# One unit fewer multiplied by seven products, and the residual rows requested in their own block

## The chip, the core and the metric
The kernel runs on one core of a Trainium2 chip. The metric is the device time of one execution in microseconds (us); the kernel before takes 782.37 us, the median of three runs (782.14 to 783.79).

## What is computed
Two graph layers over 4096 nodes with 256 features. `adj` is a dense 4096x4096 float32 matrix, and each layer multiplies all of it.

```
deg  = sum(adj, axis=1, keepdims=True) + 1e-5
out0 = relu((adj / deg) @ x @ W_neigh.T + b_neigh + x @ W_self.T + b_self)
x1   = layernorm(x + out0)
d    = rowsum(adj) ** -0.5                      # 0 where the sum is 0
out1 = relu((d[:, None] * adj * d[None, :]) @ x1 @ W + b)
out  = layernorm(x1 + out1)
```

## The kernel before, in words
Each layer is cut into `NB = 8` blocks of 512 output rows. A block is a sum over the 4096 nodes, taken in `NU = 16` units of 256 nodes. For a unit the queue of SyncE (SP) requests a tile of the transposed matrix, `raw`, 128x1024 float32 (512 KB), into a ring of four slots. ScalarE (ACT) rounds it to `hi`, VectorE (DVE) takes `lo = raw - hi` and TensorE (PE) multiplies in three passes: hi by hi, hi by the low part of the features, lo by hi. The sums of block b stand in `ps_main[b % 2]`. In the second layer the features are `z`, the scaled rows of the first layer; they lie in `zs` for the first 28 tiles and in `xs` for the last four.

A plain unit is 12 matmuls of 512 columns (L1079). In blocks 1 to 6 of the second layer the units in `SU` are multiplied another way (`seven_products`, L994): a unit is read as a 2x2 arrangement of quarters, and seven products of quarter sums replace eight products. That makes 21 matmuls of 256 columns: nine at L1017 on `hi`, `lo` and precomputed sums of the features, and twelve at L1026 on sums of the quarters of `raw`. Those sums cost work on DVE and ACT:

- `s_sums` and `s_last_sum`: four additions over 128x256 on DVE (L738, L739, L741, L745). They stand two units ahead of the unit that they serve, so that the sums for unit 3 are made in unit 1.
- `s_hi`: the rounding of the sums on ACT (128x1024, L359, shown as `xs<-acc`), and `s_lo`: their low part on DVE (L567, `xs<-acc,xs`).
- Of `raw` itself only three quarters are split (128x768 in place of 128x1024).
- Once, in block 0 of the second layer: `t_sums`, `t_hi`, `t_lo` make the feature sums for two units at a time, at units 5, 8, 11 and 14 for seven units.

Some of the products belong to two quarters; they gather in `ps_epi` and are joined to the columns in the next block. There, while PE works on units 0 to 4, ACT copies them out (`take_own`, L382, after unit 2's `hi`), DVE makes four additions (`join_own`, L690 to L697) and one over 128x1024 (`join_columns`, L704), ACT rounds the joined columns (`st_hi`), and DVE takes their low part (`st_lo`). In DVE's program `join_columns` stands ahead of unit 3's `lo`, and `st_lo` right behind it. PE's product with the weights of the block before (L958) stands behind unit 3 and again behind unit 5. The rest of the block before (bias, residual, layer norm, store) follows in units 6 to 15; its store is issued by ACT in unit 15. In the code a block's epilogue is always run inside the next block.

Everything on an engine runs in program order. Waits are on semaphores that only count up. SP requests the tile of unit u once DVE has made the `lo` of unit u - 4 (`l_ready`), ACT makes the `hi` of unit u once PE is done with unit u - 4 (`unit_done`). The residual rows of a block, 512 KB from DRAM into `res`, are requested by `load_residual` (L281): at unit 2 of the next block, behind that unit's tile and ahead of the tile of unit 3. In the second layer the request waits until the first layer's eight stores have landed. `res` is read in units 6 to 9 of the next block.

Of the kernel before, what the change touches and what calls it, by code (L numbers as in the profile page):

```python
# [29 lines left out]
NB = N // IB  # L30
TB = IB // P
UJ = 2
NU = JT // UJ
# [4 lines left out]
ZOWN = JT - TB  # L38
# [1 line left out]
HT = TB // 2  # L40
TAIL = NU - RING
WARM = 10
SU = tuple(range(1, 14, 2))
NS = len(SU)
SUMS_AT = tuple(max(u - 2, 0) for u in SU)
SRING = 2
T_AT = XC + FH
T_UNITS = tuple(range(5, 16, 3))
S_AT = T_AT + 2 * NS
QP = 32  # L50
QS = IB // QP
# [5 lines left out]
def build(nc, x_nat, xt_in, adj_in, wn_in, bn_in, ws_in, bs_in, w1_in, b1_in, out):  # L57
    f32 = mybir.dt.float32
    f32r = mybir.dt.float32r
    bf16 = mybir.dt.bfloat16  # L60
    ALU = mybir.AluOpType
# [4 lines left out]
    with ctx:  # L66
        def sb(name, shape, dt=f32):
            return ctx.enter_context(nc.sbuf_tensor(name, shape, dt))

        def sem(name):  # L70
            return ctx.enter_context(nc.semaphore(name))
# [4 lines left out]
        zs = sb("zs", [P, ZOWN, 2, F], f32r)  # L76
# [47 lines left out]
        z_joined, t_chain, t_ready = sem("z_joined"), sem("t_chain"), sem("t_ready")  # L124
# [5 lines left out]
        tt_stored = sem("tt_stored")  # L130
# [20 lines left out]
        def slot(u):  # L151
            return u % RING

        def is_last(e):

            return isinstance(e, int) and e == NB - 1

        def is_first(b):
            return isinstance(b, int) and b == 0
# [5 lines left out]
        def x_stage(c):  # L165

            if c == 0:
                return acc[:, 1, :].rearrange("p (t f) -> p t f", t=XC)
            return (res, tt)[c % 2][:, :, :]

        def w_stage(i):

            return acc[:, 1, i * IB:(i + 1) * IB].rearrange("p (k f) -> p k f", k=FH)

        def wait_x_split(eng, c):

            eng.wait_ge(xl_ready, c + 1)
# [14 lines left out]
        def by_seven(layer, b):  # L192

            return layer == 1 and not isinstance(b, int)
# [14 lines left out]
        def s_index(b, parity, u):  # L209

            return b * NS + (SU.index(u) - NS)

        def s_slot(parity, u):

            return ((0 if parity == 1 else NS) + SU.index(u)) % SRING

# [40 lines left out]
        @block.sync  # L257
        def _(sp):
            def load_x(c):
                if c >= 3:  # L260
                    wait_x_split(sp, c - 2)
                sp.dma_start(x_stage(c), x_nat[c]).then_inc(x_full[c % 2], 16)

            def load_weights():
                sp.wait_ge(unit_done, WHOLE)
                wait_x_split(sp, 0)
                sp.dma_start(w_stage(1), ws_in).then_inc(ws_full, 16)
                sp.dma_start(w_stage(0), wn_in).then_inc(wn_full, 16)

            def load_biases():  # L270
                for dst, src in ((bias0, bn_in), (bias1, b1_in)):
                    sp.dma_start(dst[:, :], src.rearrange("(a n) -> a n", a=1).to_broadcast([P, F]))\
                      .then_inc(bias_full, 16)

            def load_xt(b, u):
                if u != (9 if is_first(b) else 3):
                    return

                sp.dma_start(xt[:, :, :], xt_in[b]).then_inc(xt_full, 16)

            def load_residual(layer, e):  # L281


                if layer == 1:
                    sp.wait_ge(tt_stored, (NB + 1) * 16)
                rows = x_nat[e] if layer == 0 else x1_dram[e].rearrange("t p f -> p t f")
                sp.dma_start(res[:, :, :], rows).then_inc(res_full, 16)

            def one_block(layer, b, parity, epi):
                g0 = b * NU + layer * NB * NU  # L290
                for u in range(NU):
                    if epi is None and u == 0:
                        sp.dma_start(raw[:, 0, :], adj_in[0, 0]).then_inc(raw_full[0], 16)
                        continue
                    if not (epi is None and u < RING):

                        if epi is None and u - RING < WHOLE:
                            sp.wait_ge(unit_done, u - RING + 1)
                        else:
                            sp.wait_ge(l_ready, g0 + (u - RING + 1))  # L300
                        if layer == 0 or (is_first(b) and u < RING):
                            sp.wait_ge(acc_done, g0 + (u - RING + 1))
                    sp.dma_start(raw[:, slot(u), :], adj_in[b, u]).then_inc(raw_full[slot(u)], 16)
                    if layer == 0:
                        load_xt(b, u)
                    if epi is None:
                        if u % 2 == 1 and 1 < u < NU - 1:
                            load_x((u + 1) // 2)
                        if u == 8:
                            load_weights()  # L310
                        if u == 12:
                            load_biases()
                    elif layer == 1 and is_last(b) and u == 8:

                        sp.wait_ge(c_ready, NB - 1)
                        sp.dma_start(w1_raw, w1_in[:, FH - 1, :]).then_inc(w1_full, 16)
                    elif u == 2:
                        load_residual(*epi)
                        if layer == 1 and is_first(b):

                            sp.dma_start(xt[:, :, 0:F], w1_in).then_inc(w1_full, 16)

            def last_epilogue(epi):
                load_residual(*epi)
                for t in range(HT):
                    sp.wait_ge(x1_ready, (2 * NB - 1) * TB + t + 1)
                    sp.dma_start(out[NB - 1, t], tt[:, t, :]).then_inc(tt_stored, 16)
                sp.wait_ge(y_ready, 1)
                sp.dma_start(out[NB - 1, HT], tt[:, HT, :]).then_inc(tt_stored, 16)

                sp.wait_ge(tt_stored, (2 * NB + TB) * 16)

            layers(sp, one_block, last_epilogue)

        @block.gpsimd
# [20 lines left out]
        def _(act):  # L356
# [21 lines left out]
            def take_own(e, parity):  # L378

                act.wait_ge(own_zeroed, 1)  # L380
                act.wait_ge(unit_done, (e + NB) * NU + (SU[-1] + 1))
                act.activation(own_sbuf[:, :, :], ps_epi[:, parity * HT:(parity + 1) * HT, :], ACT.Copy).then_inc(own_ready, 1)  # L382
# [8 lines left out]
            def s_hi(b, parity, u):  # L391
                act.wait_ge(s_ready, s_index(b, parity, u) + 1)
                split_hi(s_part(0, parity, u), acc[:, s_slot(parity, u), :]).then_inc(sh_ready, 1)
# [48 lines left out]
            def one_block(layer, b, parity, epi):  # L442
                g0 = b * NU + layer * NB * NU
                k0 = b * (NU // RING) + layer * NB * (NU // RING)
                for u in range(NU):
# [25 lines left out]
                    if not (epi is None and u < RING):  # L471
                        act.wait_ge(unit_done, g0 + (u - RING + 1))
                    by_7 = by_seven(layer, b) and u in SU
                    cols = slice(0, UW - HB if by_7 else UW)
# [5 lines left out]
                    if by_7:  # L480
                        s_hi(b, parity, u)
                    if layer == 1 and is_first(b) and u in T_UNITS:
                        t_hi(T_UNITS.index(u))
                    if epi is not None:
# [68 lines left out]
        def _(dve):  # L553
# [152 lines left out]
            def t_sums(j):  # L706

                gs = t_group(j)
                m = len(gs)
                tiles = zs[:, 4 * gs[0]:4 * gs[-1] + 4].rearrange("p (g i) c f -> p g i c f", i=4).bitcast(f32)  # L710
                z = acc[:, 0, 0:m * IB].rearrange("p (g q f) -> p g q f", q=UJ, f=F)
                t = acc[:, 1, 0:m * IB].rearrange("p (g k f) -> p g k f", k=4, f=P)
                b11, b12, b21, b22 = z[:, :, 1, 0:P], z[:, :, 1, P:F], z[:, :, 0, 0:P], z[:, :, 0, P:F]
                t1, t2, t3, t4 = [t[:, :, k, :] for k in range(4)]
                dve.tensor_tensor(z, tiles[:, :, 2:4, 0, :], tiles[:, :, 2:4, 1, :], ALU.add).then_inc(z_joined, 1)
                dve.wait_ge(z_joined, j + 1)
                dve.tensor_tensor(t3, b22, b12, ALU.subtract).then_inc(t_chain, 1)
                dve.tensor_tensor(t1, b12, b11, ALU.subtract).then_inc(t_chain, 1)
                dve.wait_ge(t_chain, 3 * j + 1)
                dve.tensor_tensor(t2, t3, b11, ALU.add).then_inc(t_chain, 1)  # L720
                dve.wait_ge(t_chain, 3 * j + 3)
                dve.tensor_tensor(t4, b21, t2, ALU.subtract).then_inc(t_ready, 1)
# [71 lines left out]
            def one_block(layer, b, parity, epi):  # L794
# [8 lines left out]
                for u in range(NU):  # L803
# [26 lines left out]
                    if layer == 1 and is_first(b):  # L830
                        if u in T_UNITS:
                            t_lo(T_UNITS.index(u))
                        if u + 1 in T_UNITS:
                            t_sums(T_UNITS.index(u + 1))
                        if u == NU - 1:
# [340 lines left out]
```

## Time and profile before

| | us |
|---|---|
| median of 3 runs | 782.37 |
| profiled execution, its own time | 785.61 |
| its span in the trace | 783.9 |
| PE busy | 771.1 (98%) |
| DVE busy | 706.4 (90%) |
| ACT busy | 424.9 (54%) |

The span runs from the first to the last instruction; 1.7 us of the profiled execution lie around it. The granted TensorE clock is full (a mean of 0.997) except at the two ends. Matmuls are pipelined, so the duration of one (391 ns for 512 columns) is longer than the distance between the starts of two. How long a unit takes on PE is read from start to start. The second layer begins on PE near 401 us; its blocks take some 46 us each.

### The profile page before, as it was taken

How to read it: one execution, taken by the hardware profiler on the slowest of the kernel's cores; microseconds unless marked ns; L12 is line 12 of the kernel's file. 1: busy time of each engine (PE TensorE's matmuls, PEld its weight loads, DVE VectorE, ACT ScalarE, POOL GpSimd, SP SyncE). 2: the span in 40 equal slices, each digit the busy share in tenths (PEclk: the TensorE clock that was granted, in tenths of full speed). 3: DMA queues.
4: the chain of work that ended last, by engine and by line, in shares of the span. 5: the costliest groups of instructions: out<-in, count | busy, mean ns of one | idle time of the engine just before them, and what ended most of it. 6: DMA issues, size and time to landing. Idle time of an engine off the chain costs nothing.

```text
span 783.9 us, 12545 instructions
## 1 busy us (share of the span) xinstructions
PE 771.1 (98%) x4106; PEld 661.3 (84%) x4106; DVE 706.4 (90%) x1193; ACT 424.9 (54%) x590; POOL 2.5 (0%) x14
## 2 busy tenths in 40 slices
PE   9999999999999999999999999999999999999996
PEld 6888888888888888888888789798888989898886
DVE  6999999999899998998979899798989989898654
ACT  5644644646356463454535756556565665657452
POOL 0000000000000000000000000000000000000000
PEclk9999999999999999999999999999999999999998
DMA  7966574756647456474674556658465574847741
GB/s 300 335 231 202 199 253 156 248 190 202 226 161 247 171 201 237 142 247 177 199 242 145 197 176 208 216 164 267 161 214 209 186 245 162 268 161 215 259 149 54
DMA packets 54205, 161.08 MB, mean 205 GB/s; under 512 B 5024, under 2 KB 18080, under 8 KB 54176
## 3 DMA queue, kind: packets, MB, share of 16 engines
q1 hardware_dynamic: 45680, 151.54, 57.4%
q10 hardware_dynamic: 8352, 9.05, 3.4%
q8 instruction: 16, 0.26, 0.1%
q0 software_dynamic: 144, 0.13, 0.1%
q14 instruction: 13, 0.11, 0.1%
HBM read 152.31 MB, written 8.39 MB: 205 GB/s over the span
## 4 chain that ended last, share of the span: by engine, by line
PE 55%; DVE 25%; issue 10%; DMA 5%; ACT 4%; DVEq 1%; ACTq 0%; SPq 0%
PE ps_main L1079 45%; DVE lo L567 7%; PE ps_epi L958 6%; DVE xs L567 5%; DMA raw<-adj_t 3%; ACT hi L359 2%; DVE acc L741 2%; DVE acc L848 1%; PE ps_main L1101 1%; DVE tt L623 1%; DVE acc L738 1%; DVE ps_main L704 1%; DVE tt L639 1%; DMA tt<-x_nat 1%; ACT tt L406 1%
## 5 line engine op out<-in xcount | busy, mean ns | idle before, releaser
L359 ACT ACTIVATE hi<-raw 128x1024 fp32r<-128x1024 f32 x254 | 255.5, 1018 | 147.6 <-PE ps_main L1079 98.6
L567 DVE TENSOR_TENSOR lo<-raw,hi 128x1024 fp32r<-128x1024 f32 x254 | 297.4, 1174 | 29.0 <-ACT hi L359 28.9
L1079 PE MATMUL ps_main<-hi,xs 128*128 128x512 f32 x1120 | 278.9, 391 | 0.4 <-DVE xs L681 0.4
L1079 PEld LDWEIGHTS ps_main<-hi,xs 128*128 128x128 f32 x1120 | 207.3, 188 | 42.5 <-DVE xs L681 0.8
L1079 PE MATMUL ps_main<-lo,xs 128*128 128x512 f32 x560 | 149.7, 389 | 0.0
L848 DVE TENSOR_TENSOR acc<-acc,raw 128x1024 f32<-128x1024 f32 x112 | 136.3, 1217 | 0.0
L1079 PE MATMUL ps_main<-hi,zs 128*128 128x512 f32 x544 | 135.6, 391 | 0.0
L1079 PEld LDWEIGHTS ps_main<-lo,xs 128*128 128x128 f32 x560 | 105.1, 188 | 21.9
L1079 PEld LDWEIGHTS ps_main<-hi,zs 128*128 128x128 f32 x544 | 99.5, 188 | 18.9
L359 ACT ACTIVATE xs<-acc 128x1024 fp32r<-128x1024 f32 (+1 forms) x47 | 49.3, 1049 | 73.0 <-DVE acc L745 60.7
L1079 PE MATMUL ps_main<-lo,zs 128*128 128x512 f32 x272 | 72.7, 389 | 0.0
L567 DVE TENSOR_TENSOR xs<-acc,xs 128x1024 fp32r<-128x1024 f32 (+1 forms) x47 | 56.7, 1206 | 6.9 <-ACT xs L359 6.9
L1026 PE MATMUL ps_epi<-xs 128*128 128x256 f32 x378 | 62.5, 283 | 0.0
L1079 PEld LDWEIGHTS ps_main<-lo,zs 128*128 128x128 f32 x272 | 51.1, 188 | 10.6
L1026 PEld LDWEIGHTS ps_epi<-xs 128*128 128x128 f32 x378 | 54.3, 192 | 0.0
L406 ACT ACTIVATE tt<-tt,nmr,inv_root 128x256 f32<-128x256 f32 x60 | 32.6, 591 | 26.6 <-DVE nmr L676 26.6
L1026 PE MATMUL ps_main<-xs,zs 128*128 128x256 f32 x126 | 36.8, 292 | 2.8 <-ACT xs L359 1.5
L400 ACT ACTIVATE ps_epi<-tt,nmean 128x256 f32<-128x256 f32 x48 | 22.5, 468 | 29.9 <-DVE nmean L645 29.9
L359 ACT ACTIVATE st_hi<-ps_main 128x1024 fp32r<-128x1024 f32 (+1 forms) x18 | 16.5, 919 | 36.5 <-DVE ps_main L704 26.5
L1026 PEld LDWEIGHTS ps_main<-xs,zs 128*128 128x128 f32 x126 | 24.1, 191 | 5.0 <-DVE xs L567 2.5
L639 DVE SCALAR_TENSOR_TENSOR tt<-tt,res 128x256 f32<-128x256 f32 x64 | 26.5, 417 | 0.0
L567 DVE TENSOR_TENSOR st_lo<-ps_main,st_hi 128x1024 fp32r<-128x1024 f32 (+1 forms) x18 | 19.6, 1090 | 7.3 <-ACT st_hi L359 6.9
(157 smaller groups left out, 784.8 us busy)
## 6 DMA issues: line engine op xcount, KB each, us to landing
raw<-adj_t SPq DMA_DIRECT2D x256, 512.0 KB, 3.5
res<-x_nat SPq DMA_DIRECT2D x11, 512.0 KB, 6.1
xt_sb<-xt SPq DMA_DIRECT2D x8, 512.0 KB, 6.4
x_scratch<-tt ACTq DMA_DIRECT2D x8, 512.0 KB, 4.1
res<-x_scratch SPq DMA_DIRECT2D x8, 512.0 KB, 6.1
out<-tt ACTq DMA_DIRECT2D x7, 512.0 KB, 7.4
tt<-x_nat SPq DMA_DIRECT2D x3, 512.0 KB, 4.6
acc<-x_nat ACTq DMA_DIRECT2D x1, 512.0 KB, 4.9
```

The lines of the kernel that those rows point to most:

```text
L359: return act.activation(dst, src, ACT.Copy)
L400: act.activation(tile_sums(layer, e, parity, t)[:, 0:F], tt[:, t, :], ACT.Square, bias=nmean[:, t:t + 1], accum_out=squares[:, t:t + 1]).t ...
L406: act.activation(tt[:, t, :], tt[:, t, :], ACT.Identity, bias=nmr[:, t:t + 1], scale=rstd[:, t:t + 1]).then_inc(x1_ready, 1)
L567: return dve.tensor_tensor(dst, src, hi_part.bitcast(f32), ALU.subtract)
L623: ins = dve.scalar_tensor_tensor(out=tt[:, t, :], in0=sums[:, 0:F], scalar=(rdeg, d_cur)[layer][:, t:t + 1], in1=(bias0, bias1)[layer][:, ...
L639: link(dve.scalar_tensor_tensor(out=tt[:, t, :], in0=tt[:, t, :], scalar=0.0, in1=res[:, t, :], op0=ALU.max, op1=ALU.add, accum_out=sums[: ...
L704: dve.tensor_tensor(columns, columns, own, ALU.add).then_inc(c_ready, 1)
L741: dve.tensor_tensor(s2, a22, s3, ALU.subtract).then_inc(s_chain, 1)
L848: dve.tensor_tensor(a, a, raw[:, slot(v), :], ALU.add).then_inc(acc_done, 1)
L958: last = pe.matmul(ps, st[:, k, rows], weight(part, k), start=(k == 0 and q == 0), stop=(k == FH - 1 and q == 2))
L1026: last = pe.matmul(ps, st(part), mov[:, at * HB:(at + 1) * HB], start=(ps is p5 and first and i == 0), stop=(n > 0 and last_s and i == 2), ...
L1079: last = pe.matmul(ps[:, f, :], stationary(layer, part, jt, f), mov[:, slot(u), cols], start=(jt == 0 and i == 0), stop=(jt == JT - 1 and ...
```

## The change
Unit 3 leaves `SU`, so that six units of a block go by seven products and unit 3 is plain. `SUMS_AT` follows from `SU`: no sums are made in unit 1 any more. The feature sums have three groups of two units (5, 8, 11) and no fourth, and `t_sums` picks its tiles by the units in `SU`, which are no longer evenly spaced. In the second layer the residual rows of block b are requested at unit 14 of block b itself, behind the tile of unit 14 and ahead of the tile of unit 15. In block 0 that request waits for seven of the first layer's stores, not eight. The last block's rows too are requested at its unit 14.

```diff
-SU = tuple(range(1, 14, 2))
+SU = (1, 5, 7, 9, 11, 13)
-T_UNITS = tuple(range(5, 16, 3))
+T_UNITS = tuple(range(5, 5 + 3 * ((NS + 1) // 2), 3))
...
-            def load_residual(layer, e):
+            def load_residual(layer, e, stored=NB):
                 if layer == 1:
-                    sp.wait_ge(tt_stored, (NB + 1) * 16)
+                    sp.wait_ge(tt_stored, (stored + 1) * 16)
...
-                    elif u == 2:
+                    if layer == 1 and u == NU - 2:
+
+                        load_residual(layer, b, NB - 1 if is_first(b) else NB)
+                    elif u == 2 and epi is not None and epi[0] == 0:
                         load_residual(*epi)
-                        if layer == 1 and is_first(b):
+                        if layer == 1:
                             sp.dma_start(xt[:, :, 0:F], w1_in).then_inc(w1_full, 16)
             def last_epilogue(epi):
-                load_residual(*epi)
...
-                tiles = zs[:, 4 * gs[0]:4 * gs[-1] + 4].rearrange("p (g i) c f -> p g i c f", i=4).bitcast(f32)
+                first, last = SU[gs[0]] * UJ, SU[gs[-1]] * UJ
+                step = last - first if m == 2 else UJ
+                at = 0 if first + m * step <= ZOWN else step - UJ
+                tiles = zs[:, first - at:first - at + m * step].rearrange("p (g i) c f -> p g i c f", i=step)\
+                    .bitcast(f32)[:, :, at:at + UJ]
...
-                dve.tensor_tensor(z, tiles[:, :, 2:4, 0, :], tiles[:, :, 2:4, 1, :], ALU.add).then_inc(z_joined, 1)
+                dve.tensor_tensor(z, tiles[:, :, :, 0, :], tiles[:, :, :, 1, :], ALU.add).then_inc(z_joined, 1)
```

On DVE, at the start of a block of the second layer's loop, from unit 1's `s_lo` (`xs<-acc,xs`) on, before:

```order
L567 TENSOR_TENSOR xs<-acc,xs 128x1024
L738 TENSOR_TENSOR acc<-raw 128x256
L739 TENSOR_TENSOR acc<-raw 128x256
L740 ISA
L741 TENSOR_TENSOR acc<-raw,acc 128x256
L744 REGISTER_ALU
L745 TENSOR_TENSOR acc<-raw,acc 128x256
L821 REGISTER_ALU
L567 TENSOR_TENSOR lo<-raw,hi 128x1024
L690 TENSOR_TENSOR xt_sb<-xt_sb 128x256
L692 ISA
L693 TENSOR_TENSOR xt_sb<-xt_sb 128x256
```

The same place now (`xt_sb` is where the joined products are gathered; L692 is the first of the four additions of the join):

```order
L569 TENSOR_TENSOR xs<-acc,xs 128x1024
L827 REGISTER_ALU
L569 TENSOR_TENSOR lo<-raw,hi 128x1024
L692 TENSOR_TENSOR xt_sb<-xt_sb 128x256
L694 ISA
L695 TENSOR_TENSOR xt_sb<-xt_sb 128x256
L697 TENSOR_TENSOR xt_sb<-xt_sb 128x256
```

The four sums for unit 3, which read the tile of unit 3, are gone from between `s_lo` of unit 1 and `lo` of unit 2.

On SP, in the block ahead of the second layer's loop (block 0), from the first residual request on, before:

```order
L287 DMA res<-x_nat 128x1024
L321 DMA xt_sb<-w 128x2x256
L303 DMA raw<-adj_t 128x1024 x13
L251 UNCONDITIONAL_BRANCH
L251 ISA
```

The same place now:

```order
L287 DMA res<-x_nat 128x1024
L324 DMA xt_sb<-w 128x2x256
L303 DMA raw<-adj_t 128x1024 x12
L287 DMA res<-x_scratch 128x4x256
L303 DMA raw<-adj_t 128x1024
L251 UNCONDITIONAL_BRANCH
L251 ISA
```

The request of the block's own residual rows (`x_scratch` is the first layer's result) stands ahead of the last tile, where the loop's first block had it behind its third.

## Rows read from the trace of the kernel before

**Rows 1.** Page: busy time of PE; median landing of a tile.

```profile
PE   771.1 (98%) x4106; PEld 661.3 (84%) x4106; DVE 706.4 (90%) x1193; ACT 424.9 (54%) x590; POOL 2.5 (0%) x14
...
raw<-adj_t SPq DMA_DIRECT2D x256, 512.0 KB, 3.5
```

**Rows 2.** Timeline of PE (start, us, operation): unit 0 in blocks 1, 2, 3, 6, 7.

```profile
448.88 1.98 PE L1079 MATMUL ps_main<-hi,zs 128*128 128x512 f32 x8
...
496.16 1.98 PE L1079 MATMUL ps_main<-hi,zs 128*128 128x512 f32 x8
...
543.79 1.98 PE L1079 MATMUL ps_main<-hi,zs 128*128 128x512 f32 x8
...
681.83 1.98 PE L1079 MATMUL ps_main<-hi,zs 128*128 128x512 f32 x8
...
727.35 1.98 PE L1079 MATMUL ps_main<-hi,zs 128*128 128x512 f32 x8
```

**Rows 3.** Timeline of PE: units 12, 13, 14 of block 1 begin.

```profile
485.43 2.00 PE L1079 MATMUL ps_main<-hi,zs 128*128 128x512 f32 x8
487.27 1.07 PE L1079 MATMUL ps_main<-lo,zs 128*128 128x512 f32 x4
488.18 0.28 PE L1017 MATMUL ps_epi<-hi,zs 128*128 128x256 f32 x1
...
490.69 2.00 PE L1079 MATMUL ps_main<-hi,xs 128*128 128x512 f32 x8
```

**Rows 4.** Timeline of PE: unit 3 of block 2, product behind it; then block 6.

```profile
504.14 0.28 PE L1017 MATMUL ps_epi<-hi,zs 128*128 128x256 f32 x1
...
505.98 0.38 PE L1017 MATMUL ps_epi<-lo,zs 128*128 128x256 f32 x1 [0.97 <-DVE lo L567]
...
507.12 0.39 PE L1026 MATMUL ps_main<-xs,zs 128*128 128x256 f32 x1 [0.53 <-ACT xs L359]
...
509.15 0.40 PE L958 MATMUL ps_epi<-xs,st_hi 128*128 128x256 f32 x2
...
689.81 0.28 PE L1017 MATMUL ps_epi<-hi,zs 128*128 128x256 f32 x1
...
692.70 0.40 PE L958 MATMUL ps_epi<-xs,st_hi 128*128 128x256 f32 x2
```

**Rows 5.** Timeline of DVE: units 0 to 3 of block 2.

```profile
492.51 1.23 DVE L567 TENSOR_TENSOR lo<-raw,hi 128x1024 fp32r<-128x1024 f32 x1 [1.62 <-ACT hi L359]
...
499.54 0.42 DVE L738 TENSOR_TENSOR acc<-raw 128x256 f32<-128x256 f32 x1 [1.99 <-DMA raw<-adj_t]
...
501.01 1.22 DVE L567 TENSOR_TENSOR lo<-raw,hi 128x1024 fp32r<-128x1024 f32 x1
...
504.98 0.95 DVE L567 TENSOR_TENSOR lo<-raw,hi 128x768 fp32r<-128x768 f32 x1
506.15 1.22 DVE L567 TENSOR_TENSOR st_lo<-ps_main,st_hi 128x1024 fp32r<-128x1024 f32 x1 [0.23 <-ACT st_hi L359]
```

**Rows 6.** Chain that ended last, in order of time: tile of unit 3.

```profile
491.05 8.47 DMA raw<-adj_t
```

**Rows 7.** Timeline of SP: tile of unit 15, block 1; residual request in block 2.

```profile
481.25 0.33 SPq L303 DMA_DIRECT2D raw<-adj_t  x1
...
489.39 0.39 SPq L287 DMA_DIRECT2D res<-x_scratch  x1
```

**Rows 8.** Timeline of ACT: unit 15's hi, block 1.

```profile
488.58 1.04 ACT L359 ACTIVATE hi<-raw 128x1024 fp32r<-128x1024 f32 x1
```

**Rows 9.** Block 0's end: PE at unit 14; ACT's rounding of feature sums.

```profile
443.26 2.14 PE L1079 MATMUL ps_main<-hi,xs 128*128 128x512 f32 x8 [0.42 <-DVE xs L681]
...
438.59 0.63 ACT L359 ACTIVATE xs<-acc 128x512 fp32r<-128x512 f32 x1 [0.34 <-DVE acc L722]
```

**Rows 10.** DMA issues in 486 to 500 us (KB, us to landing).

```profile
out<-tt ACTq DMA_DIRECT2D x1, 512.0 KB, 11.3
```

**Rows 11.** The last block: SP's residual request; unit 15's hi on ACT.

```profile
755.00 0.43 SPq L287 DMA_DIRECT2D res<-x_scratch  x1
...
763.16 1.06 ACT L359 ACTIVATE hi<-raw 128x1024 fp32r<-128x1024 f32 x1 [0.68 <-PE ps_main L1079]
```

## The prediction
> **What bounds the kernel now.** I read the busy times first. PE is busy for 771.1 of 783.9 us, DVE for 706.4 [rows 1]: PE sets the time, and only two things can change it, how long PE needs for its matmuls and how long it stands still. DVE at 90% is close behind, so it can be late at single places. Next I took PE's timeline and followed the starts of unit 0 through the second layer, since a block must take the same time whenever PE is not held up. They lie at 448.88, 496.16, 543.79, 681.83 and 727.35 us in blocks 1, 2, 3, 6 and 7 [rows 2]. So block 1 takes 47.28, block 2 takes 47.63, blocks 3 to 5 together 138.04 (46.01 each), block 6 takes 45.52. The same work takes up to 2.1 us longer in one block than in another: that is standstill.
>
> Then, where it stands still. A group by seven products takes 488.18 to 490.69 = 2.51 us when nothing holds it [rows 3]. Unit 3 of block 2 starts at 504.14 and the product behind it at 509.15: 5.01 us, so 2.50 lost. PE waited for the `lo` of unit 3, then for ACT's rounding of the sums, then for their low part [rows 4]. In block 6 the same unit takes 692.70 - 689.81 = 2.89, so 0.38 lost [rows 4]. Taking that off, a block without standstill is 45.52 - 0.38 = 45.14 us. The six blocks 1 to 6 take 727.35 - 448.88 = 278.47, the floor is 6 x 45.14 = 270.84: 7.6 us are lost, by block 2.1, 2.5, then 2.6 in three blocks, and 0.4. In block 2 the loss is all in unit 3, since 47.63 - 2.50 = 45.13 is the floor again.
>
> Why DVE is late there is in its own timeline [rows 5]. Behind unit 1's work it wants the four sums for unit 3, whose tile has not landed: it stands for 1.99 us, until 499.54. The sums take it to 501.01. Then come unit 2's `lo`, the join, unit 3's `lo` at 504.98 and `st_lo` at 506.15. PE wanted that `lo` about 0.7 us after 504.14. The tile landed 8.47 us after its request at 491.05 [rows 6], against a median of 3.5 [rows 1]; ahead of it in SP's queue stood the 512 KB of residual rows, requested at 489.39 [rows 7], and beside it ran the store of the block before, which took 11.3 us [rows 10].
>
> **The change part by part.** *Unit 3 plain, cost on PE.* A plain unit takes 488.18 - 485.43 = 2.75 us, a seven-product unit 2.51 [rows 3]. Six blocks, one unit each: 6 x 0.24 = +1.4 us. It is certain, because PE has no idle time for it to hide in. The Trainium skill has a rule that would make this dearer ("TensorE: Matmul & The Clock Gate", Back-to-back issue gap: a warm matmul starts N/2.4 + 2.5 ns after the one before): 12 x 216 against 21 x 109 ns are 2.59 and 2.29 us, a difference of 0.30, so +1.8 in all, an estimate from that page. The rows of this case show 229 and 120 ns from start to start, and I go by them.
>
> *Unit 3 plain, what it takes off.* Per block DVE loses four sums, 501.01 - 499.54 = 1.47 us [rows 5], and one 1.2 us low part, and gains 0.27 (1.22 in place of 0.95 for `lo`); ACT loses one rounding. Idle time or work of DVE alone is worth nothing; what counts is when PE gets its inputs. In block 2 the sums (1.47) and the wait in front of them (1.99) fall away from between 492.51 and 506.15, so `st_lo` begins at about 506.15 - 3.46 = 502.7 and ends at 503.9. The `lo` of unit 3 is done at about 502.7. The plain unit needs its `lo` only behind its first eight matmuls, 1.84 us after its start [rows 3], so at 504.14 + 1.84 = 505.98, and the product behind it needs `st_lo` at 504.14 + 2.75 = 506.9. Both are there with 3.0 us to spare. In block 6 there is no wait to drop, only the 1.47, and it is ample for a loss of 0.38. So the standstill at unit 3 goes in all six blocks: -7.6 us. What is late next: the `lo` of unit 4 and the sums for unit 5, which now stand 3.5 us earlier as well, and PE comes to unit 4 only after a 1.4 us product. I book nothing.
>
> *The residual request moved.* In a block's first units the queue now carries tiles only, so the tile of unit 3 should land sooner than 8.47 us; nobody needs it before ACT's `hi` and DVE's `lo` of unit 3. In block 1 the request also waited for a store of the first layer, with the tile of unit 3 queued behind it; that wait goes. These are part of the 7.6 and count once. The price is at the new place: behind the request stands the tile of unit 15 and then those of the next block. In block 1 the tile of unit 15 is requested at 481.25 and ACT takes it at 488.58 [rows 7, 8]. With the request's 0.39 us in front it has 6.9 us to land without anybody noticing. The nearest rows are 3.5 at the low end and 8.47 for a tile behind residual rows and beside a store; the store is not running at unit 14, so I take 6 to 7, and a cost of nothing. If it were 8.47, `hi` and all that follows on DVE would be 1.6 us late, inside the 3.0 us of room at unit 3. The last block: its tile of unit 15 is requested just ahead of 755.00 and taken at 763.16 [rows 11], 8 us; even at 8.47 the `lo` half of that unit is not yet wanted. Nothing. The residual rows themselves land some 20 us before they are read.
>
> *The fourth group of feature sums.* It is gone from block 0: five small DVE operations, one rounding on ACT of 0.63 us that DVE held up by 0.34, and its low part. They stood ahead of the scaling of the last feature rows, for which PE waits 0.42 us at unit 14 [rows 9]. That wait goes or nearly: -0.4; at worst 0.
>
> *Sum.* -7.6 - 0.4 + 1.4 = -6.6 us in the profiled execution: 785.61 becomes 779.0. That execution is 3.2 us above the median of 782.37. The losses beyond the smallest depend on how late a tile lands, so part of the 3.2 may be standstill that ordinary runs do not have, and that the change then cannot take away. By bounds: if they have all of it, 782.37 - 6.6 = 775.8. If only block 1 keeps its 2.1 and the others have the mean of blocks 3 to 6, (2.6 + 0.4)/4 = 0.75, the loss is 5.9 and the gain 4.9: 777.5. If all six have 0.75, the loss is 4.5, the gain 3.5: 778.9. I take a gain of 5.4: **777.0 us**, with 775.3 to 779.0 as this case's own range.
>
> **Rivals.** *A: DVE stays late around the join.* The waits for tiles go, but the join chain still ends late, because ACT comes later with `take_own` or `hi` than I assume, and PE loses the 0.75 per block elsewhere in units 3 to 5. For it: DVE is at 90%, and every block without a late tile still lost something. Against it: the 1.47 us fewer are more than those losses, and a plain unit asks for its `lo` 1.1 us later. Time: -6.6 + 6 x 0.75 = -2.1, 780.3.
>
> *B: slower, by the tile of unit 15.* The residual rows go ahead of it in the same queue. If it lands L us after its request, ACT is L - 6.9 late, and DVE's whole start of the next block with it; unit 3 takes up 3.0, and the rest is PE's loss in each of six blocks. To eat up the gain of 6.6 it must lose 1.1 per block: the point is L = 11.0. At the 11.3 us that the store took in this trace [rows 10], 1.4 per block are lost, 8.4 in all: +1.8, 784.2. Against it: that store is another kind of transfer, at the fullest moment of the block, and tiles behind residual rows took 8.47 there. The Trainium skill says that descriptors are consumed in ring order on each DMA engine ("DMA: Bandwidth & Descriptors", Queues, rings and completion order), so the later tile has to let the rows through first; the trace's 8.47 us is in line with it.
>
> *C: no change.* DVE's lateness was only where it showed, and PE, freed at unit 3, meets it again later in the block, at units 13 to 15, say. Then of the 7.6 all but the 1.4 for the plain unit comes back: within 1 us, 781.5 to 783.4. Against it: behind unit 3 PE never waited, though DVE was 2 to 3 us later than it will be.
>
> **How the numbers follow.** Main case 0.80, A 0.11, B 0.04, C 0.05. What a measurement of this kernel can tell from no change is about 0.2%, 1.6 us, so faster begins below 780.8. The main case is faster throughout; A is on the faster side but near the bound, 0.07 to 0.04 between faster and same; C is same (0.04) or slower (0.01), B slower. Faster 0.87, same 0.08, slower 0.05. The range of 775.2 to 780.2 takes the bounds of the main case and part of the way to A.
>
> **What would show it.** Right: the starts of unit 0 in blocks 1 to 7 lie 45.4 us apart (45.14 + 0.24), evenly; unit 3 is 12 matmuls at 2.75 us with no releaser beside it; DVE no longer waits for a tile in unit 1 or 2, and `st_lo` ends 2 to 3 us before the product. Wrong: a wait of PE at units 4 or 5 (A); hi of unit 15 released by a DMA and blocks over 46 us (B); waits of PE near the end of the block (C); or a median gain of under 3 us with even blocks in the profile, which would say that ordinary runs did not have the loss.

## The result: 0.56% faster, and the profile after

The changed kernel takes 778.91 us, the median of 5 runs (778.44 to 779.27), against 782.35 for the kernel before, measured beside it: a ratio of 0.9944 with a 95% interval of 0.9932 to 0.9957. In a later session the kernel before took 784.33 us and the changed one 778.54, a ratio of 0.9928 (0.9914 to 0.9942). The changed kernel hardly varies; the one before does.

The profiled execution went from 785.61 to 778.69 us, its span from 783.9 to 777.0. From the page of the changed kernel, busy times and the chain that ended last:

```profile
PE 769.2 (99%) x4052; PEld 659.7 (85%) x4052; DVE 692.2 (89%) x1157; ACT 425.1 (55%) x583; POOL 2.5 (0%) x14
...
PE 99%; DVE 0%; ACT 0%; issue 0%
```

In the page of the kernel before that chain reads:

```profile
PE 55%; DVE 25%; issue 10%; DMA 5%; ACT 4%; DVEq 1%; ACTq 0%; SPq 0%
```

PE's timeline after the change, unit 0 of blocks 0, 1, 2, 3 and 7 of the second layer, which answers to [rows 2]:

```profile
401.74 1.98 PE L1085 MATMUL ps_main<-hi,zs 128*128 128x512 f32 x8
...
448.41 1.98 PE L1085 MATMUL ps_main<-hi,zs 128*128 128x512 f32 x8
...
493.75 1.98 PE L1085 MATMUL ps_main<-hi,zs 128*128 128x512 f32 x8
...
539.09 1.98 PE L1085 MATMUL ps_main<-hi,zs 128*128 128x512 f32 x8
...
720.45 1.98 PE L1085 MATMUL ps_main<-hi,zs 128*128 128x512 f32 x8
```

Blocks 1 to 6 all take 45.34 us, to the hundredth: 720.45 - 448.41 = 272.04 for the six, against 278.47 before. That is 6.43 of the 6.9 us. Block 0 takes 46.67; before it began at 401.45 and took 47.43, so another 0.76. The first layer ended 0.3 later; it is the same in every kernel here and ends between 401.4 and 402.8 us, so that is chance.

DVE's timeline in units 0 to 3 of block 2, which answers to [rows 5], and the start of PE's unit 3 and of the product behind it, for [rows 4]:

```profile
487.31 1.23 DVE L569 TENSOR_TENSOR lo<-raw,hi 128x1024 fp32r<-128x1024 f32 x1 [1.62 <-ACT hi L361]
...
496.29 1.22 DVE L569 TENSOR_TENSOR lo<-raw,hi 128x1024 fp32r<-128x1024 f32 x1
497.48 1.22 DVE L569 TENSOR_TENSOR st_lo<-ps_main,st_hi 128x1024 fp32r<-128x1024 f32 x1
```

```profile
501.73 1.98 PE L1085 MATMUL ps_main<-hi,zs 128*128 128x512 f32 x8
...
504.45 0.40 PE L964 MATMUL ps_epi<-xs,st_hi 128*128 128x256 f32 x2
```

The tile of unit 15, now behind the residual rows in the queue, landed like this in block 1 (KB, us from issue), which answers to [rows 7]:

```profile
raw<-adj_t SPq DMA_DIRECT2D x1, 512.0 KB, 6.7
```

`st_lo` is done at 498.7, 5.8 us before PE's product wants it; I had worked out 3.0. The difference stands at the block's start: DVE begins unit 0 at 487.31, 6.4 us ahead of PE (493.75). Before, it was 3.65 ahead (492.51 and 496.16) [rows 2, 5]. DVE did not only get rid of work in unit 1, it came into the block earlier.

### The profile page after: what moved, and what is told of

The parts are those of the page before. It is cut to its first block, busy times and chain, and to the rows that moved or that the text cites. A ratio compares the mean times of both kernels' runs of the same rounds, so it can differ in the third digit from the quotient of the medians.

```text
span 777.0 us, 12364 instructions
## 1 busy us (share of the span) xinstructions
PE 769.2 (99%) x4052; PEld 659.7 (85%) x4052; DVE 692.2 (89%) x1157; ACT 425.1 (55%) x583; POOL 2.5 (0%) x14
## 4 chain that ended last, share of the span: by engine, by line
PE 99%; DVE 0%; ACT 0%; issue 0%
PE ps_main L1085 75%; PE ps_epi L964 7%; PE ps_epi L1032 5%; PE ps_main L1023 3%; PE ps_main L1032 2%; PE ps_epi L1023 2%; PE ps_main L1107 1%; PE ps_main L964 1%; PE ps_main L1060 1%; PE ps_main L1045 1%; PE ps_epi L1117 0%; DVE tt L625 0%; PE ps_epi L985 0%; DVE tt L641 0%; ACT ps_epi L513 0%; ACT tt L527 0%
## 5 line engine op out<-in xcount | busy, mean ns | idle before, releaser
L361 ACT ACTIVATE hi<-raw 128x1024 fp32r<-128x1024 f32 x254 | 260.6, 1028 | 215.0 <-PE ps_main L1085 150.3
L1085 PE MATMUL ps_main<-hi,zs 128*128 128x512 f32 x592 | 147.4, 391 | 0.0
L1085 PEld LDWEIGHTS ps_main<-hi,zs 128*128 128x128 f32 x592 | 108.5, 188 | 20.9
L1085 PE MATMUL ps_main<-lo,zs 128*128 128x512 f32 x296 | 79.1, 389 | 0.0
L569 DVE TENSOR_TENSOR xs<-acc,xs 128x1024 fp32r<-128x1024 f32 x40 | 48.9, 1221 | 7.1 <-ACT xs L361 7.1
L361 ACT ACTIVATE xs<-acc 128x1024 fp32r<-128x1024 f32 x40 | 42.1, 1053 | 23.5 <-DVE acc L751 11.3
L1032 PE MATMUL ps_epi<-xs 128*128 128x256 f32 x324 | 53.4, 283 | 0.0
L1032 PEld LDWEIGHTS ps_epi<-xs 128*128 128x128 f32 x324 | 46.7, 192 | 0.0
L1032 PE MATMUL ps_main<-xs,zs 128*128 128x256 f32 x108 | 30.6, 283 | 0.0
L964 PE MATMUL ps_epi<-ws_sb,st_hi 128*128 128x256 f32 x128 | 23.6, 282 | 0.0
```

Source lines behind the costliest of these rows:

```text
L361: return act.activation(dst, src, ACT.Copy)
L569: return dve.tensor_tensor(dst, src, hi_part.bitcast(f32), ALU.subtract)
L964: last = pe.matmul(ps, st[:, k, rows], weight(part, k), start=(k == 0 and q == 0), stop=(k == FH - 1 and q == 2))
L1032: last = pe.matmul(ps, st(part), mov[:, at * HB:(at + 1) * HB], start=(ps is p5 and first and i == 0), stop=(n > 0 and last_s and i == 2), ...
L1085: last = pe.matmul(ps[:, f, :], stationary(layer, part, jt, f), mov[:, slot(u), cols], start=(jt == 0 and i == 0), stop=(jt == JT - 1 and ...
```

## The experiments

**The kernel before, profiled again.** It is unchanged.

> The kernel before, unchanged, profiled once more: its first profile was 785.61 us, its ordinary runs are 782.3. Theory T: what the ordinary runs do not have is standstill at unit 3 for late tiles. Then this profile shows blocks 1 to 6 of the second layer 45.1 us plus a loss of 0.4 to 1 us each (2.1 in block 1), about 4.5 in all, not 7.6, and a span near 780.7. Rival: the 3.3 us lay elsewhere (start, first layer), and the loss at unit 3 is 7.6 again with a shorter span.

Measured: 783.24 us, span 781.5. Units 0 of blocks 1 and 7:

```profile
449.09 1.98 PE L1079 MATMUL ps_main<-hi,zs 128*128 128x512 f32 x8
...
725.00 1.98 PE L1079 MATMUL ps_main<-hi,zs 128*128 128x512 f32 x8
```

275.91 us for six blocks, so 5.1 lost over 6 x 45.14 in place of 7.6. The 2.5 us less are the 2.4 that this execution is faster than the first profile. I had expected about 4.5 us of loss and a span near 780.7. So the two executions differ by the standstill in these blocks, and the first profile had caught much of it. But the ordinary runs beside this one had a median of 784.52 us (783.47 to 785.02): it lies 1.3 us below them, where the first profile lay 3.2 above its own. And the standstill is not all that varies: the first layer's end moves by up to 1.4 us, and kernels whose blocks are even in the profile still have runs up to 2.2 us apart (below).

**The request alone, and the plain unit alone.** The first undoes the change of `SU` (and with it the groups of feature sums), the second undoes the move of the request.

```diff
 # seven_units_res_moved, against the changed kernel
-SU = (1, 5, 7, 9, 11, 13)
+SU = (1, 3, 5, 7, 9, 11, 13)
 # plain_res_at_unit_2, against the changed kernel
-                    if layer == 1 and u == NU - 2:
-                        load_residual(layer, b, NB - 1 if is_first(b) else NB)
-                    elif u == 2 and epi is not None and epi[0] == 0:
+                    if u == 2 and epi is not None:
                         load_residual(*epi)
...
             def last_epilogue(epi):
+                load_residual(*epi)
```

> The residual request alone is moved; unit 3 stays with seven products. Theory T (DVE's sums for unit 3 in unit 1 keep it late at the join): PE still waits 0.4 to 0.75 us in unit 3 of each block; against the changed kernel -1.4 for the cheaper unit, +0.4 for the feature sums, +2.4 to 4.5 of standstill: 780.3 to 782.4. Rival R (the standstill came from the late tile, so the moved request alone does it): no waits, blocks 45.1 us apart, 777.9.

> Unit 3 is plain, the residual request stays at unit 2 of the next block. Theory T: without sums in unit 1 nobody needs the tile of unit 3 before DVE has joined, so a late tile is hidden; blocks 45.34 us apart, 778.9 as the changed kernel. Rival R (the late tile is the cause): one or two blocks still lose 1 to 2 us, block 1 among them, 780 to 782.

| kernel | median us | ratio to before (784.52) | blocks 1 to 6, us each |
|---|---|---|---|
| request moved, unit 3 by seven | 781.02 | 0.9957 (0.9944 to 0.9971) | 45.30, 45.55, 45.87, 45.54, 45.83, 45.53 |
| unit 3 plain, request at unit 2 | 778.85 | 0.9931 (0.9917 to 0.9944) | 45.34 in all six |

The plain unit alone does everything: every block at 45.34, and the same time as the whole change. A tile is still late in its block 1, where ACT stands 2.1 us for it, and costs nothing. The request alone is worth 3.5 us in the kernel with seven units, chiefly in block 1 (45.30 us, against 46.86 in the repeated profile), where SP had waited 6.5 us in the first profile for a store of the first layer, and nothing that can be seen once the unit is plain. The two were one gain, not two. With the request moved DVE waits for no tile any more, and yet five of the six blocks lose 0.4 to 0.7 us: that part was never a matter of tiles.

**One more plain unit.** `SU = (1, 5, 9, 11, 13)`.

> The changed kernel with unit 7 plain too (five units by seven products). Theory T: PE sets the time everywhere, so each further plain unit costs 0.23 us in each of six blocks: blocks 45.57 us apart, 778.9 + 1.4 = 780.3. Rival: DVE is still part of the bound somewhere and its relief pays for it, 778.9 or less.

Measured: 779.88 us (778.87 to 780.81), all six blocks 45.52 us. Theory T holds and prices the exchange: 0.18 us per unit and block (I had expected 0.23), where 0.20 separates 45.34 from the 45.14 of a block with seven products in seven units and no wait (below). The single rows of one unit had given 0.24 [rows 3].

**More work on DVE.** Four, then three reductions ahead of unit 2's `lo`, their result unused.

```diff
+                        for i in range(4 if by_seven(layer, b) and u == 2 else 0):     # 3 in the other
+                            dve.tensor_reduce(spare[:, i:i + 1], raw[:, slot(u), :], AX.X, ALU.add)
                         split_lo(lo[:, slot(u), cols], raw[:, slot(u), cols], hi[:, slot(u), cols]).then_inc(l_ready, 1)
```

> The changed kernel with four reductions over 128x1024 (some 1.15 us each, result unused) on DVE ahead of unit 2's lo in blocks 1 to 6: 4.6 us more in front of the join. By the prediction's 3.0 us of room PE loses 1.6 us in each of six blocks: 788. By the 5.8 us of the changed kernel's trace it loses nothing at unit 3: 779, at most 781 if DVE, then busy for 44.5 of 45.3 us, comes late elsewhere.

> The changed kernel with three reductions (3.4 us) on DVE ahead of unit 2's lo in place of four. Theory L (DVE is bound by its own round: 40.0 us of work a block and 3.1 us of waits that its order forces, so 43.1 in 45.34, and whatever is over 45.34 lengthens the block): 40.0 + 3.1 + 3.4 = 46.5, so blocks of 46.5 us, 1.2 more each, 786. Theory S (room at the join, 5.8 us by the trace): no loss, 779. The prediction's 3.0 us of room: 0.4 a block, 781.3.

Measured: 790.89 us with four (1.0083, 1.0068 to 1.0099) and 783.66 with three (0.9992, 0.9981 to 1.0004). Neither room was right. With 4.6 us more, less than the 5.8 of room, the first block lost 1.2 us and the others 2.1 to 2.4; with three the first lost nothing and the others 1.0 to 1.3. The first block lives on the lead it brings along; after that each block is a round that DVE can't finish in time. To see this I took DVE's own rounds, from the start of unit 0's `lo` to the same place one block later, here from block 3 to block 4. The columns are length, PE, PEld, DVE, ACT, POOL, granted clock, DMA share, GB/s, for the kernel before, the changed one, three more, four more:

```profile
540.44:585.96 45.52, 45.29 (x279) 40.61 (x278) 42.07 (x79) 27.51 (x39) 0.00 (x0) 1.00 0.62 202
```

```profile
532.82:577.81 44.99, 44.99 (x270) 40.15 (x269) 39.99 (x73) 27.62 (x37) 0.00 (x0) 1.00 0.64 207
```

```profile
537.07:583.37 46.30, 45.53 (x270) 40.06 (x269) 43.11 (x76) 26.78 (x38) 0.00 (x0) 1.00 0.63 202
```

```profile
539.35:586.79 47.44, 45.84 (x270) 39.99 (x269) 44.25 (x78) 26.78 (x38) 0.00 (x0) 1.00 0.61 199
```

And what DVE waited for in block 3 of the kernel before:

```profile
DVE lo L567 <- ACT hi L359: 2.5, 2, 1.6
DVE xs L567 <- ACT xs L359: 0.3, 1, 0.3
DVE st_lo L567 <- ACT st_hi L359: 0.2, 1, 0.2
```

Length less DVE's work is 3.45, 5.00, 3.19 and 3.19 us. In the two slowed kernels and in the one before it is what DVE has to wait in any case, some 3 us at places where its order makes it wait for ACT (two of them at units 15 and 0, where ACT is busy with the block's norm and its store), and a few tenths between instructions. Only in the changed kernel is it more, because there DVE waits for PE as well: its rounds of 45.0 and 45.5 us alternate around PE's 45.34, and its lead at the block's start stays at 6.3 to 6.6 us. In every other round one of the waits for ACT is 0.3 us longer, so that rounds of two lengths alternate: 45.52 and 45.85 us with seven units and the request moved, 46.30 and 46.65 with three reductions, 47.4 and 47.8 with four. These are the lengths of PE's blocks too. So the kernel before was on DVE's round even in the blocks with no late tile, and a late tile was added to the round directly: the rounds that hold a wait for a tile of 1.99 and of 0.7 us take 47.93 and 46.65 us. Theory L gave 46.5 for three; measured 46.3 to 46.65, though its total of 786 forgot the first block's lead.

**Two more transfers in front of the tile of unit 15.**

```diff
                         load_residual(layer, b, NB - 1 if is_first(b) else NB)
+                        for i in range(2):
+                            sp.dma_start(spare[i, b], x_nat[b]).then_inc(spare_full, 16)
```

> The changed kernel with two further 512 KB copies (DRAM to DRAM, of rows of x, read by nobody) behind the residual request at unit 14 of each block of the second layer, ahead of the tile of unit 15. That is rival B on purpose: the tile, which now lands in 6.7 us, should land in 11 to 13. By the prediction's room (6.9 us unnoticed, then 3.0 at unit 3) blocks 1 to 6 are 1 to 3 us longer, 785 to 797. By the room that the changed kernel's trace shows (low part of the joined columns done 5.8 us before PE's product) the blocks stay within 0.3 us of 45.34: 779 to 781.

Measured: 778.92 us (777.74 to 779.97), every block at 45.34. The tile was late for ACT, which waited 2.0 us for it in block 1:

```profile
486.36 1.06 ACT L367 ACTIVATE hi<-raw 128x1024 fp32r<-128x1024 f32 x1 [2.00 <-DMA raw<-adj_t]
```

but it landed 7.2 us after its own request at 479.06, itself held back by the others. Counted from 0.65 us after the residual request at 476.54, where the change alone puts it, that is some 9 us, not 11 to 13. So the run shows that about 2 us of lateness there cost nothing, and does not tell my two rooms apart. Rival B is far from the changed kernel, whose tile landed in 6.7 us.

**Back to seven units, in another order.** Against the kernel with seven units and the request moved: at unit 3 ACT and DVE take the sums of the unit before the joined columns; the four groups of feature sums stand where `T_UNITS` says.

```diff
-T_UNITS = tuple(range(5, 5 + 3 * ((NS + 1) // 2), 3))      # (5, 8, 11, 14) for seven units
+T_UNITS = (5, 8, 10, 12)      # seven_units_all_hidden; also (3, 5, 8, 11) and (4, 6, 8, 11)
 ACT:
+                    if by_7:
+                        s_hi(b, parity, u)
                     if epi is not None and epi[0] == 1 and u == 3:
                         joined_columns(epi[1], 1 - parity)
-                    if by_7:
-                        s_hi(b, parity, u)
 DVE:
+                    if by_seven(layer, b) and u == 3:
+                        s_lo(b, parity, u)
                     place(u, 1)
                     if by_seven(layer, b):
-                        if u in SU:
+                        if u in SU and u != 3:
                             s_lo(b, parity, u)
```

> Seven units and the moved request, with one order changed at unit 3: ACT rounds the sums of unit 3 before the joined columns, DVE takes their low part before that of the joined columns. Theory: what is left of the standstill in that kernel (0.2 to 0.7 us a block) is PE waiting for the low part of the sums behind st_lo; then it goes, blocks 45.14 us apart: 781.0 - 2.8 = 778.2. Rival: DVE is simply full at the block's start, and the wait turns up at the product behind unit 3 or at the next units: 780.5 to 781.

> As the one before, and the four groups of feature sums at units 5, 8, 10 and 12 of block 0 in place of 5, 8, 11 and 14. Theory: block 0 of the second layer is 47.4 us long with a group at unit 14 and 46.67 without; with the group earlier it is 46.67 again: 0.7 less than the one before, 777.5, and 1.4 under the changed kernel. Rival: the groups crowd DVE in units 8 to 12 of block 0 and PE waits there: no gain.

> Seven units, request moved, the sums of unit 3 taken first, and the four groups of feature sums at units 3, 5, 8 and 11 of block 0, so that none stands in front of the norm of the last rows. Theory: blocks 1 to 6 at 45.14 to 45.3, block 0 at 46.67 with no wait for the last z rows: 777.4 to 777.9, at least 1 us under the changed kernel. Rival: a group at unit 3 meets the first layer's last block there, and PE waits in units 3 to 5 of block 0: 778.5 or more.

> The same with groups at units 4, 6, 8 and 11. Theory: as the one before, 777.4 to 777.9. Rival: three groups two units apart cost DVE 6.4 us in each pair of units of 5.4 us, and its lead runs out by unit 8: a wait of PE of 1 us or more in block 0.

> The changed kernel once more, beside the other kernels of this chip: 778.9, blocks 1 to 6 at 45.34 us, block 0 at 46.67.

| kernel | median us | ratio to before of its session | block 0 | blocks 1 to 6 |
|---|---|---|---|---|
| sums first, groups 5, 8, 11, 14 | 779.13 | 0.9932 (0.9918 to 0.9946) | 47.41 | 45.14 to 45.52 |
| groups 5, 8, 10, 12 | 781.94 | 0.9968 (0.9957 to 0.9979) | 50.90 | 45.14 |
| groups 3, 5, 8, 11 | 777.59 | 0.9916 (0.9902 to 0.9930) | 46.67 | 45.14 |
| groups 4, 6, 8, 11 | 777.57 | 0.9916 (0.9902 to 0.9930) | 46.67 | 45.13 to 45.34 |
| the changed kernel again | 778.54 | 0.9928 (0.9914 to 0.9942) | 46.66 | 45.34 |

The order alone takes away most of the standstill: in the first of these block 3 is 45.17 us long with the same seven units, against 45.85 in the kernel before:

```profile
539.45:584.62 45.17, 45.17 (x280) 40.81 (x279) 41.95 (x79) 27.61 (x39) 0.00 (x0) 1.00 0.67 212
```

PE no longer waits there behind `st_lo` for the sums' low part, and DVE no longer waits 0.2 us for `st_hi`. The six blocks lose 0.55 us together in place of 2.8; I had booked the whole 2.8, and 778.2 us. What is left has the same reason as before. DVE's rounds are shorter by 0.3 us only, 45.2 and 45.5 in turn, which is still more than the 45.14 that PE needs. The kernel with groups 3, 5, 8, 11 hides this, since DVE comes into block 2 with a lead of 5.5 us in place of 3.6. DVE's unit 0 in its blocks 2 and 7 (PE's stand at 493.65 and 719.35):

```profile
488.13 1.23 DVE L569 TENSOR_TENSOR lo<-raw,hi 128x1024 fp32r<-128x1024 f32 x1 [1.62 <-ACT hi L361]
...
714.81 2.36 DVE L569 TENSOR_TENSOR lo<-raw,hi 128x1024 fp32r<-128x1024 f32 x2 [1.64 <-ACT hi L361]
```

Over five rounds the lead falls from 5.5 to 4.5 us: DVE needs 45.34 us a round, PE takes 45.14. In the kernel with sums first and groups 5, 8, 11, 14 the blocks begin to lose at a lead near 3.2 us. By my estimate, from 5.5 at 0.2 a round, this one would be there after some twelve rounds, and seven units would then be no better than six, whose blocks take 45.34 as well.

The feature sums were a matter of place: at unit 14 they cost 0.75 us and part of DVE's lead; at units 10 and 12, where I had expected 777.5 us, they pushed the first layer's last norm back and PE stood still for 2.4 us; early in the block they cost nothing. The last three rows come from one chip. Seven units in this order, with the groups early, are the fastest kernel of the study, by 0.95 us of median over the changed one; the intervals overlap, but the blocks show where it comes from, 6 x 0.20 = 1.2 us.

## Why the prediction was right, and where not

The forecast was 777.0 us (775.2 to 780.2); measured 778.91. The gain of the profiled execution, 6.9 us, was forecast as 6.6; that of ordinary runs, 3.4, as 5.4.

- *Unit 3 plain, +1.4.* Right in kind, a little large: +1.2, from 45.14 to 45.34 in six blocks. The formula of the Trainium skill ("TensorE: Matmul & The Clock Gate", Back-to-back issue gap) would have made it 1.8; the blocks do not agree. The Trainium skill gives that formula there for one matmul by itself and says that at 512 columns it counts too much, which I had left out. The rows of this case have it the other way: 229 ns from start to start against its 216 [rows 3].
- *The standstill at unit 3, -7.6.* It went entirely in the profiled execution: PE waits at no unit of blocks 1 to 6. The sum came out, but only in part for the reason that I gave: see the cause below.
- *Sizing it for ordinary runs.* This is the term that was off. I put the gain between 3.5 and 6.6 and took 5.4; in the first session it was 3.4, just under my lower bound. (The 775.3 at the lower end of this case's own range follows from none of the bounds; the lowest that I worked out is 775.8.) The loss over the floor was 5.1 us in the repeated profile, and in the ordinary runs of the first session, by 3.4 + 1.2 - 0.76, some 3.9. In the later session, with 5.8 us of gain, it would by the same sum be 6.2; no profile of these ordinary runs shows it. One profile of this kernel is a sample of something that varies by 2 us and more.
- *The cause of the lateness.* Half right. I named the late tile and, with it, the moved request as part of the 7.6. The tile explained what came on top in blocks 1, 2 and 4, where DVE waited 1.9, 2.0 and 0.7 us for it, but the plain unit alone gives all the gain. "Idle time or work of DVE alone is worth nothing" failed: DVE's round was the bound in these blocks, 42.1 us of work and some 3.5 to 3.8 of waits and gaps that its order forces. With unit 3 plain the work is 40.0 us a round, 2.1 less (I had 2.4), and the wait for `st_hi` goes. That brought the round under PE's 45.34 us, with room for a late tile besides, and was the change's whole effect. The order of the work was worth nearly as much, as the last experiment shows.
- *3.0 us to spare at unit 3.* Measured 5.8, since I shortened DVE's path inside one block and left its start where it was. And neither number is room for more work, as the added reductions show.
- *The request at its new place, 0.* Right as to its cost; it gained nothing either. The tile landed in 6.7 us (I took 6 to 7, with 6.9 unnoticed), and two more transfers changed nothing.
- *The fourth group of feature sums, -0.4.* -0.76: the wait at unit 14 went [rows 9], and the block ends in step.
- *Rival A* described the kernel with only the request moved: DVE late around the join, 0.2 to 0.7 us a block. It does not hold for the changed kernel. *Rivals B and C* did not occur.

## What to carry to other kernels

An engine at 90% beside one at 98% can be the bound of a loop: take its own round, from one of its instructions to the same one a pass later, add its forced waits to its work, and compare with the round's length. If they meet, work taken off it shortens the round, and so does an order in which it waits for less, until another engine sets the time. A lead measured at one place of a loop is not room for more work in every pass; and if the lead shrinks from pass to pass, the engine is the slower one, even where nothing has waited for it yet. Where a kernel's runs vary and its successor's do not, profile the first one twice before booking the difference.

## What the hardware showed that I had not expected

With the groups at units 10 and 12, PE stood still in block 0 for some 2.5 us, and the eight matmuls behind took 3.43 us from start to start in place of 1.84 [rows 3]:

```profile
445.41 3.59 PE L1087 MATMUL ps_main<-hi,xs 128*128 128x512 f32 x8 [2.40 <-DVE xs L683]
```

The busy times of 446 to 449 us show the reason, a granted clock of 0.56 where all stretches around it have 0.87 to 1.00, so mostly the lower level, 1.2 GHz:

```profile
446.00:449.00 3.00, 3.00 (x9) 2.39 (x8) 3.00 (x7) 0.18 (x1) 0.00 (x0) 0.56 0.73 277
```

The wait of 2.5 us cost 1.6 more in clock. Behind the waits of 0.2 to 1.0 us in block 2 of the kernel before the granted clock stayed at 1.00.
